# Softmax pieces of the first attention spread differently over sixteen heads, in a fused two-layer block

## The chip, the cores and the metric

One Trainium2 chip, one of its cores. The metric is the device time of the whole kernel in microseconds (us): the median of several executions. The engines of the core run side by side: TensorE (PE) with its weight load (PEld), VectorE (DVE), ScalarE (ACT), GpSimd (POOL) and SyncE (SP), which only issues DMAs here.

## The reference

Four stages follow one another on x of 8 x 256 tokens with 256 numbers each: a cross attention, a mixture of 64 experts, a second cross attention and a mixture of 8 experts. Each adds its gated result to x. The change lies in the first attention only:

```python
x = x + jnp.tanh(g_xattn[0]) * _L0_xattn_ref(_layernorm(x, axis=-1), ctx_1024, ...)
# in _L0_xattn_ref: 16 heads, D = 128, 64 keys for each of the 8 sequences
q = (hidden_states @ Wq).reshape(B, Sq, H, D)
k = (encoder_hidden_states @ Wk).reshape(B, Skv, H, D)
v = (encoder_hidden_states @ Wv).reshape(B, Skv, H, D)
q = rmsnorm(q, gq)
k = rmsnorm(k, gk)
scores = jnp.einsum('bqhd,bkhd->bhqk', q, k) * scale
attn = jax.nn.softmax(scores, axis=-1)
out = jnp.einsum('bhqk,bkhd->bqhd', attn, v)
return out.reshape(B, Sq, H * D) @ Wo
```

## The kernel before

The 2048 tokens are 16 tiles of 128; four tiles (512 tokens, two sequences) are a group, and there are four groups. `step(i)` works on group i of the first attention, i = 0 to 3. It is written once for each engine, and the engines meet at semaphores. In step i, PE, DVE, ACT and POOL make the queries and scores of group i, head by head, and between the heads the softmax, transposes and output of group i - 1. So step 0 has no softmax in it, steps 1, 2 and 3 have, and the softmax of group 3 comes after step 3 in a loop of its own, which the change leaves alone.

A head h of the loop, engine by engine, each in the order of its own program:

- PE: the q product of head h (six matmuls of 512 columns, line 1742) into one of two banks, which is free when DVE has copied head h - 2. Then, in heads that the table `turns` names, eight transposes of a tile's softmax (`transpose_attn`, line 1690), and in heads that `outs` names the output product of a tile (`output`, line 1697). Then the scores of head h - 2 (line 1727) and its row of the sum of squares (line 1718), for which POOL must have split the squares.
- DVE: the copy of the head's queries out of the bank (`qT`, line 725), then the pieces that the table `pieces` names for this head. Head 12 also has `row_stats` of the next group, head 15 `row_roots` (not in step 3).
- ACT: two squares of `qT` (lines 1372 and 1376), behind the copy; then, by its tables, `attn_out` (line 1326: two banks of transposes to `attnT`) and `exponential` (line 1322); in odd heads from 3 on it takes scores out (line 1364).
- POOL: `q2_lo`, the difference of the two squares, one subtraction a head (line 486).

The pieces of a tile j on DVE, for its 128 x 1024 scores (16 heads of 64 keys): `by_norm` (line 659: times the inverse norm), `maximum` (664), `shift` (668: less the maximum), then ACT's exponential, `sums` (673 and 675: sum and reciprocal), `divide` (682: writes `prob`, which is one buffer, so that divide j waits for the transposes of tile j - 1), and `out` (645: adds the output product to x). After the divide come PE's transposes, ACT's `attn_out` and PE's output product, and then `out`. The output product uses one bank, so output j waits for out j - 1.

The order is written out by hand in the three tables; each engine does its work in just that order, and what stands behind a waiting instruction waits too. After the sixteen heads, PE makes the last output, the keys of the next group, and its values, which ACT evacuates (lines 1315 to 1317); then the tokens of the next group are transposed, and the next step begins.

Of the kernel before, what the change touches and what calls it, by code (L numbers as in the profile page):

```python
# [101 lines left out]
def flamingo(nc, a, out, stages=4):  # L102
    with ExitStack() as ctx:
# [454 lines left out]
        def _(dve):  # L558
# [148 lines left out]
            def step(i, first_, last):  # L707
                qr.at(Q_PREP, Q_STEP, i)
                ch.at(PREP_CHAIN + STEP_CHAIN * i - (0 if first_ else SOFT_CHAIN))
                by_norm, maximum, shift, sums, divide = softmax_pieces(i - 1, (i + 1) % 2)  # L710
                t0 = T_PREP + T_STEP * i - T_HEADS + (0 if last else 2)

                def out(j):
                    residual(i - 1, j, one_bank=True)


                pieces = {0: (by_norm, 0, maximum, 0), 1: (shift, 0, by_norm, 1), 2: (maximum, 1, shift, 1),
                          3: (sums, 0), 4: (divide, 0), 5: (sums, 1), 6: (divide, 1, by_norm, 2),
                          7: (maximum, 2, shift, 2, out, 0), 8: (by_norm, 3, maximum, 3), 9: (sums, 2),
                          10: (divide, 2, out, 1), 11: (shift, 3), 13: (sums, 3), 14: (divide, 3, out, 2)}  # L720
                if not first_:

                    dve.wait_ge(s_ring.free, S_PREP + S_STEP * (i - 1) + 8)
                for h in range(H0):
                    dve.tensor_copy(qT[:, h % 3, :], qr.read(dve)[:]).then_inc(q_ring.free, 1)  # L725
                    if not first_:
                        run = pieces.get(h, ())
                        for piece, j in zip(run[0::2], run[1::2]):
                            if piece is divide:
                                divide(j, t0 + 2 * j if j else None)  # L730
                            else:
                                piece(j)
                    if h == 12 and not last:
                        row_stats(i + 1)
                    if h == 15 and not last:
                        row_roots(EPS0)
                dve.wait_ge(q_norm, 2 * i + 1)
                dve.tensor_copy(n_rows[:], n_bank[0:H0, :]).then_inc(n_copied, 1)
                if not last:
                    keys_in()  # L740
                if not first_:
                    out(3)
                dve.wait_ge(q_norm, 2 * i + 2)
                ch.add(dve.tensor_scalar(qvar[:], n_bank[:, 0:G * H0], 1.0 / D0, EPS0, ALU.mult, ALU.add))
                if not last:

                    row_apply(i + 1)
                    key_norm(1)
                    split_tokens(i + 1)
                ch.wait()  # L750
                inverse_root(rq[:], qvar[:], G * H0)
                assert first_ or last or ch.k == STEP_CHAIN, (ch.k, STEP_CHAIN)
# [535 lines left out]
        def _(act):  # L1288
# [66 lines left out]
            def step(i, first_, last):  # L1355
                qr.at(Q_PREP, Q_STEP, i)
                sr.at(S_PREP, S_STEP, i)
                tr.at(T_PREP - (0 if first_ else T_HEADS), T_STEP, i)
                if not last:
                    context_in((i + 1) % 2)  # L1360

                def scores_out(pair):
                    b = sr.read(act)
                    act.activation(raw[:, i % 2, :, 2 * pair * SKV:2 * (pair + 1) * SKV],
                                   b[:].rearrange("p (j n) -> p j n", j=G), ACT.Copy).then_inc(s_ring.free, 1)


                exps, outs = {2: 0, 3: 1, 8: 2, 12: 3}, {5: 0, 8: 1, 12: 2, 15: 3}
                for h in range(H0):
                    qr.skip(1)  # L1370
                    qr.evacuated(act)
                    act.activation(q2_hi[:, h % 3, :], qT[:, h % 3, :], ACT.Square)  # L1372

                    if not (first_ and h < 2):
                        act.wait_ge(q2_split, H0 * i + h - 1)
                    act.activation(q2[h % 2], qT[:, h % 3, :], ACT.Square).then_inc(q2_ready, 1)  # L1376
                    if not first_ and h in outs:
                        attn_out(outs[h])
                    if not first_ and h in exps:
                        exponential(i - 1, exps[h], (i + 1) % 2)  # L1380
                    if h >= 3 and h % 2:
                        scores_out((h - 3) // 2)
                scores_out(H0 // 2 - 1)
                values_in()
                if not last:
                    tokens_in()
                    keys_in()
# [235 lines left out]
        def _(pe):  # L1623
# [77 lines left out]
            def step(i, first_, last):  # L1701
                qr.at(Q_PREP, Q_STEP, i)
                sr.at(S_PREP, S_STEP, i)
                tr.at(T_PREP - (0 if first_ else T_HEADS), T_STEP, i)
                if not last:
                    context_in(i + 1)
                pe.wait_ge(xnT_ready, i + 1)
                s_bank = [None]

                def scores(h, done):  # L1710
                    qr.evacuated(pe, done - h)
                    pe.wait_ge(q2_split, H0 * i + h + 1)
                    place = [(h ^ 1) if j >= 2 else h for j in range(G)]
                    for half in range(2):
                        at, row = slice(half * 2 * P, (half + 1) * 2 * P), place[2 * half]

                        for n, v in enumerate((q2_hi, q2_lo)):
                            mm = pe.matmul(n_bank[0:H0, at], band_r[:, H0 - 1 - row:2 * H0 - 1 - row],  # L1718
                                           v[:, h % 3, at], start=(h == half == n == 0),
                                           stop=(h == H0 - 1 and half == n == 1))  # L1720
                    if h == H0 - 1:
                        mm.then_inc(q_norm, 1)
                    if h % 2 == 0:
                        s_bank[0] = sr.fill(pe)
                    for j in range(G):
                        at = (2 * j + place[j] % 2) * SKV
                        mm = pe.matmul(s_bank[0][:, at:at + SKV], qT[:, h % 3, j * P:(j + 1) * P],  # L1727
                                       kT[:, h, (j // 2) * SKV:(j // 2 + 1) * SKV], start=True, stop=True)
                    if h % 2:
                        mm.then_inc(s_ring.full, 1)  # L1730


                turns, outs = {5: 0, 8: 1, 12: 2, 15: 3}, {6: 0, 9: 1, 13: 2}
                for h in range(H0):
                    b = qr.fill(pe)
                    if first_ and h % 4 == 0:
                        pe.wait_ge(wq_split, h // 4 + 1)

                    terms = [(w, v, c) for c in range(C) for w, v in (
                        (wq_hi, xnT_top), (wq_hi, xnT_rest), (wq_lo, xnT_top))]  # L1740
                    for n, (w, v, c) in enumerate(terms):
                        mm = pe.matmul(b[:], w[:, c, h * D0:(h + 1) * D0], v[:, c, :],  # L1742
                                       start=(n == 0), stop=(n == len(terms) - 1))
                    mm.then_inc(q_ring.full, 1)
                    if not first_ and h in turns:
                        transpose_attn(i - 1, turns[h])
                    if not first_ and h in outs:
                        output(i - 1, outs[h])
                    if h >= 2:
                        scores(h - 2, h + 1)  # L1750
                scores(H0 - 2, H0)
                scores(H0 - 1, H0)
                if not first_:
                    output(i - 1, G - 1)
                if not last:
                    keys()
                pe.wait_ge(n_copied, i + 1)
                pe.sem_inc(pe_wait_done, 1)
                for j in range(G):
                    mm = pe.transpose(n_bank[:, j * H0:(j + 1) * H0], n_rows[:, j * P:(j + 1) * P],  # L1760
                                      ident[0:H0, 0:H0])
                mm.then_inc(q_norm, 1)
                values(i % 2)
                if not last:
                    transpose_xn(i + 1)
                    transpose_keys(i + 1)
# [371 lines left out]
```

## Time and profile before

| | |
|---|---|
| time, median of 3 runs | 1227.14 us (1225.15 to 1227.94) |
| the profiled execution | 1225.4 us, span 1223.6 us |
| PE busy | 951.2 us, 78% of the span |
| DVE busy | 727.4 us, 59% |
| ACT busy | 433.1 us, 35% |
| POOL busy | 279.2 us, 23% |
| heads of step 1, 2, 3 | about 100.5 to 162, 187 to 249, 273 to 335 us |

Times are counted from the start of the span. Matmuls overlap, so one instruction's duration is longer than the distance to the next one's start; distances are what an engine needs for a stretch. An idle time in brackets is that of the engine just before the instruction, with what released it. PEclk is the clock granted to TensorE, 1.00 being the full 2.4 GHz.

### The profile page before, as it was taken

The numbers are of one execution on the slowest core, as the hardware profiler recorded it, in microseconds if no ns is written. First come the engines' busy times: TensorE is split into PE (matmuls) and PEld (weight loads), VectorE is DVE, ScalarE is ACT, GpSimd is POOL, SyncE is SP. The second block draws the span as 40 slices with busy tenths as digits, with TensorE's granted clock in tenths as the row PEclk, the third lists the DMA queues.
The fourth block names the chain that finished last, engine by engine and source line by source line (L and its number), as shares of the span: only waits on it lengthen the run. The fifth ranks groups of instructions, "written<-read, shape, count | busy, mean of one in ns | idle before, by whom it ended". The sixth has DMA issues, their size and how long they took to land.

```text
span 1223.6 us, 16469 instructions
## 1 busy us (share of the span) xinstructions
PE 951.2 (78%) x5499; PEld 791.0 (65%) x5499; DVE 727.4 (59%) x1697; ACT 433.1 (35%) x811; POOL 279.2 (23%) x225
## 2 busy tenths in 40 slices
PE   5998989989977530566776756777868999999998
PEld 3876867867856320455665633443547989999898
DVE  7267567668378889322222367988986545444343
ACT  4556454455463320111111103445364233332322
POOL 0423303304200000378888730001100000000000
PEclk8999998999989765687878867888869999999899
DMA  8004000000000114388878656000000000000000
GB/s 291 4 1 148 2 1 1 1 1 1 1 0 1 44 58 106 75 185 166 179 172 183 128 130 216 1 3 1 1 1 1 1 6 13 2 17 0 18 1 18
DMA packets 58945, 66.48 MB, mean 54 GB/s; under 512 B 5069, under 2 KB 55687, under 8 KB 58119
## 3 DMA queue, kind: packets, MB, share of 16 engines
q1 hardware_dynamic: 45236, 46.45, 12.1%
q0 software_dynamic: 12288, 18.88, 8.8%
q8 instruction: 36, 0.59, 0.2%
q10 hardware_dynamic: 1363, 0.37, 0.1%
q14 instruction: 22, 0.18, 0.0%
HBM read 48.13 MB, written 17.56 MB: 54 GB/s over the span
## 4 chain that ended last, share of the span: by engine, by line
PE 46%; DVE 20%; issue 14%; POOL 7%; ACT 6%; DMA 5%; ACTq 0%; DVEq 0%; PEldq 0%; POOLq 0%; PEld 0%; SPq 0%
PE bank L2044 12%; PE bank L2070 7%; DMA acc<-y,dst_now 4%; PE bank L1742 4%; PE bank L1697 4%; POOL acc L507 3%; PE bank L1727 3%; POOL xg L497 2%; PE bank L2055 2%; PE bank L1931 2%; POOL q_lo L486 2%; DVE cand L922 2%; DVE keyT L925 2%; PE bank L1718 2%; DVE small L1067 1%
## 5 line engine op out<-in xcount | busy, mean ns | idle before, releaser
L2044 PE MATMUL bank<-gu_hi,xnT_split 128*128 128x352 f32 x640 | 164.0, 330 | 4.9 <-DVE soft L1238 3.7
L486 POOL TENSOR_TENSOR q_lo<-soft,q_hi 128x512 fp32r<-128x512 f32 x64 | 93.2, 1456 | 237.1 <-ACT soft L1376 237.0
L2044 PEld LDWEIGHTS bank<-gu_hi,xnT_split 128*128 128x128 f32 x640 | 114.6, 192 | 5.6 <-DVE soft L1238 4.0
L507 POOL DMA_INDIRECT acc<-y,dst_now x64 | 102.5, 1602 | 27.8 <-issue 20.4
L2044 PE MATMUL bank<-gu_lo,xnT_split 128*128 128x352 f32 x320 | 104.5, 327 | 0.0
L1238 DVE SCALAR_TENSOR_TENSOR soft<-sg,combine_w,bank 128x176 f32<-128x176 f32 x160 | 56.5, 395 | 70.0 <-PE bank L2044 64.5
L725 DVE COPY qT<-bank 128x512 f32<-128x512 f32 x64 | 44.2, 691 | 88.5 <-PE bank L1742 87.4
L497 POOL DMA_INDIRECT xg<-table,src_now x64 | 63.9, 999 | 127.8 <-DVE src_now L955 108.6
L975 DVE TENSOR_SCALAR y<-bank,xg 128x256 f32<-128x256 f32 x64 | 28.0, 480 | 105.0 <-PE bank L1859 105.0
L1586 ACT ACTIVATE sg<-bank 128x352 f32<-128x352 f32 x80 | 37.0, 464 | 127.3 <-PE bank L2044 123.3
L1846 PEld LDWEIGHTS bank<-xgT,w_gu 128*88 128x88 f32 x512 | 75.9, 194 | 7.4 <-issue 5.3
L1846 PE MATMUL bank<-xgT,w_gu 128*88 128x128 f32 x512 | 77.8, 317 | 0.7 <-issue 0.7
L1832 PE MATMUL bank<-ident,xg 128*128 128x128 f32 x128 | 24.9, 327 | 65.8 <-DMA xg<-table,src_now 65.8
L1434 ACT ACTIVATE xgT<-bank 128x512 f32<-128x512 f32 x32 | 19.1, 597 | 152.2 <-PE bank L1832 152.2
L1372 ACT ACTIVATE q_hi<-qT 128x512 fp32r<-128x512 f32 x64 | 40.4, 631 | 92.1 <-DVE qT L725 91.9
L2070 PE MATMUL bank<-dn_hi,actT_hi 128*128 128x256 f32 x224 | 66.8, 298 | 0.0
L2070 PE MATMUL bank<-dn_hi,actT_lo 128*128 128x256 f32 x224 | 65.9, 294 | 0.0
L2070 PE MATMUL bank<-dn_lo,actT_hi 128*128 128x256 f32 x224 | 65.5, 293 | 0.0
L1697 PE MATMUL bank<-vw,attnT 128*128 128x256 f32 x256 | 60.3, 390 | 5.6 <-ACT attnT L1326 3.5
L1727 PE MATMUL bank<-kT,qT 128*128 128x64 f32 x512 | 64.0, 268 | 0.0
L1727 PEld LDWEIGHTS bank<-kT,qT 128*128 128x128 f32 x512 | 62.5, 191 | 1.4
L1832 PEld LDWEIGHTS bank<-ident,xg 128*128 128x128 f32 x128 | 16.8, 164 | 70.6 <-DMA xg<-table,src_now 56.7
(273 smaller groups left out, 2233.8 us busy)
## 6 DMA issues: line engine op xcount, KB each, us to landing
w_gu<-in_L_ffn_w_gu SPq DMA_DIRECT2D x32, 352.0 KB
w_dn<-in_L_ffn_w_down SPq DMA_DIRECT2D x32, 176.0 KB
acc<-zeros SPq DMA_DIRECT2D x2, 2176.0 KB, 11.9
acc_rows<-acc SPq DMA_DIRECT2D x8, 512.0 KB, 5.0
gu<-in_L_gu SPq DMA_DIRECT2D x1, 3520.0 KB, 13.5
table<-xw SPq DMA_DIRECT2D x4, 640.0 KB
wo<-in_L_xattn_Wo SPq DMA_DIRECT2D x2, 1024.0 KB, 15.1
wq<-in_L_xattn_Wq SPq DMA_DIRECT2D x1, 2048.0 KB, 17.4
```

The lines of the kernel that those rows point to most:

```text
L486: pool.tensor_tensor(q2_lo[:, h % 3, :], q2[h % 2], q2_hi[:, h % 3, :], ALU.subtract).then_inc(q2_split, 1)
L497: pool.indirect_dma_start(xg[:, q, e, :], None, table, bass.IndirectOffsetOnAxis(ap=src_now[:, q, e:e + 1], axis=0)).then_inc(xg_loaded[q] ...
L507: pool.indirect_dma_start(acc[e], bass.IndirectOffsetOnAxis(ap=dst_now[:, q, e:e + 1], axis=0), y[:, q, e, :], None, compute_op=ALU.add).t ...
L725: dve.tensor_copy(qT[:, h % 3, :], qr.read(dve)[:]).then_inc(q_ring.free, 1)
L1238: ins = dve.scalar_tensor_tensor(out=act_v[:, j % 2, at:at + F1], in0=sg[:, (j + p) % 2, e * F1:(e + 1) * F1], scalar=combine_w[:, j, 2 * ...
L1697: mm = pe.matmul(o_banks[0][:, 0:DIM], attnT[:, j % 2, p, :], vw[:, j // 2, p, :], start=(p == 0), stop=(p == 7))
L1727: mm = pe.matmul(s_bank[0][:, at:at + SKV], qT[:, h % 3, j * P:(j + 1) * P], kT[:, h, (j // 2) * SKV:(j // 2 + 1) * SKV], start=True, stop ...
L1742: mm = pe.matmul(b[:], w[:, c, h * D0:(h + 1) * D0], v[:, c, :], start=(n == 0), stop=(n == len(terms) - 1))
L1832: mm = pe.transpose(b[:, at:at + P], xg[:, q, e, c * P:(c + 1) * P], ident[:])
L1846: mm = pe.matmul(b[0:I0, e * P:(e + 1) * P], w_gu[:, q, e, c, o:o + I0], xgT[:, q % 2, e, c, :], start=(c == 0), stop=(c == C - 1))
L2044: mm = pe.matmul(b[:, 0:2 * F1], v[:, c, j * P:(j + 1) * P], w[:, c, p, o, :], start=(n == 0), stop=(n == len(terms) - 1))
L2070: mm = pe.matmul(o_banks[j % 2][:, 0:DIM], v[0:n, f, :], w[0:n, f, :], start=(f == 0 and k == 0), stop=(f == FC - 1 and k == 2))
```

## The change

Three tables are rewritten. On DVE no head from 0 to 15 is without a piece any more, and norm and maximum of tiles 1, 2 and 3 come later in part. Transposes and output product of tiles 1 and 2 come a head later: transposes 1 in head 9 in place of 8 and 2 in head 13 in place of 12, outputs 1 and 2 in heads 10 and 14 in place of 9 and 13. ACT's `attn_out` moves with the transposes, and exponentials 1 and 2 go from heads 3 and 8 to 5 and 9. The work itself is the same, instruction for instruction.

```diff
@@ DVE
-                pieces = {0: (by_norm, 0, maximum, 0), 1: (shift, 0, by_norm, 1), 2: (maximum, 1, shift, 1),
-                          3: (sums, 0), 4: (divide, 0), 5: (sums, 1), 6: (divide, 1, by_norm, 2),
-                          7: (maximum, 2, shift, 2, out, 0), 8: (by_norm, 3, maximum, 3), 9: (sums, 2),
-                          10: (divide, 2, out, 1), 11: (shift, 3), 13: (sums, 3), 14: (divide, 3, out, 2)}
+                pieces = {0: (by_norm, 0), 1: (maximum, 0, shift, 0), 2: (by_norm, 1), 3: (maximum, 1, sums, 0),
+                          4: (shift, 1, divide, 0), 5: (by_norm, 2), 6: (maximum, 2), 7: (sums, 1, out, 0),
+                          8: (divide, 1, shift, 2), 9: (by_norm, 3), 10: (maximum, 3), 11: (sums, 2, shift, 3),
+                          12: (divide, 2, out, 1), 13: (sums, 3), 14: (divide, 3), 15: (out, 2)}
@@ ACT
-                exps, outs = {2: 0, 3: 1, 8: 2, 12: 3}, {5: 0, 8: 1, 12: 2, 15: 3}
+                exps, outs = {2: 0, 5: 1, 9: 2, 12: 3}, {5: 0, 9: 1, 13: 2, 15: 3}
@@ PE
-                turns, outs = {5: 0, 8: 1, 12: 2, 15: 3}, {6: 0, 9: 1, 13: 2}
+                turns, outs = {5: 0, 9: 1, 13: 2, 15: 3}, {6: 0, 10: 1, 14: 2}
```

## Rows read from the trace of the kernel before

**Rows 1.** Windows, step 1's heads: us, busy time (instructions) of each engine, PEclk, DMA.
```profile
100.50:162.00 61.50, 59.21 (x371) 50.34 (x372) 42.16 (x66) 30.23 (x55) 24.20 (x16) 1.00 0.23 75
```

**Rows 2.** Waits of PE, one answer each for steps 1, 2, 3: total, times, longest.
```profile
PE bank L1718 <- POOL q_lo L486: 2.2, 3, 1.2
...
PE bank L1718 <- POOL q_lo L486: 1.5, 2, 1.2
...
PE bank L1718 <- POOL q_lo L486: 2.1, 3, 1.2
```

**Rows 3.** Timeline of DVE in step 1, heads 2 to 5: start, duration, operation.
```profile
110.50 1.23 DVE L668 TENSOR_TENSOR raw<-raw,small 128x1024 f32 x1
111.64 0.68 DVE L725 COPY qT<-bank 128x512 f32<-128x512 f32 x1
112.25 1.21 DVE L673 TENSOR_REDUCE small<-raw 128x16 f32 x1
...
113.86 0.69 DVE L725 COPY qT<-bank 128x512 f32<-128x512 f32 x1
114.47 1.48 DVE L682 TENSOR_TENSOR soft<-raw,small 128x1024 f32<-128x1024 f32 x1
```

**Rows 4.** Timeline of POOL in step 1, the subtractions of heads 2 and 3.
```profile
110.61 2.27 POOL L486 TENSOR_TENSOR q_lo<-soft,q_hi 128x512 fp32r<-128x512 f32 x1 [0.95 <-ACT soft L1376]
113.59 1.28 POOL L486 TENSOR_TENSOR q_lo<-soft,q_hi 128x512 fp32r<-128x512 f32 x1 [0.72 <-ACT soft L1376]
```

**Rows 5.** Timeline of PE in step 1: scores 0; in head 5, product's end, transposes 0.
```profile
105.66 0.28 PE L1718 MATMUL bank<-q_hi,band_r 128*16 128x256 f32 x1 [0.63 <-POOL q_lo L486]
...
115.52 0.39 PE L1742 MATMUL bank<-xnT_top,wq_lo 128*128 128x512 f32 x1
116.01 1.09 PE L1690 MATMUL bank<-ident,soft 128*128 128x128 f32 x8
```

**Rows 6.** Timeline of PE: starts of heads 9 to 14 and transposes 2 (head 12).
```profile
130.77 0.48 PE L1742 MATMUL bank<-xnT_top,wq_hi 128*128 128x512 f32 x1
...
137.19 0.48 PE L1742 MATMUL bank<-xnT_top,wq_hi 128*128 128x512 f32 x1
...
139.94 0.48 PE L1742 MATMUL bank<-xnT_top,wq_hi 128*128 128x512 f32 x1
...
142.67 0.48 PE L1742 MATMUL bank<-xnT_top,wq_hi 128*128 128x512 f32 x1
...
144.14 1.03 PE L1690 MATMUL bank<-ident,soft 128*128 128x128 f32 x8
...
146.30 0.48 PE L1742 MATMUL bank<-xnT_top,wq_hi 128*128 128x512 f32 x1
...
152.51 0.48 PE L1742 MATMUL bank<-xnT_top,wq_hi 128*128 128x512 f32 x1
```

**Rows 7.** Timeline of DVE in step 1: out 1, copies 11 and 12, row statistics.
```profile
140.59 0.48 DVE L645 SCALAR_TENSOR_TENSOR x<-bank,gates,x 128x256 f32 x1
141.60 0.69 DVE L725 COPY qT<-bank 128x512 f32<-128x512 f32 x1 [0.53 <-PE bank L1742]
...
144.34 0.69 DVE L725 COPY qT<-bank 128x512 f32<-128x512 f32 x1 [0.92 <-PE bank L1742]
144.95 1.40 DVE L595 BATCH_NORM_STATS2 stats<-x 128x6 f32 x4
146.49 0.38 DVE L599 BATCH_NORM_AGGREGATE mv<-stats 128x2 f32<-128x6 f32 x4
```

**Rows 8.** Timeline of ACT in step 1, head 12: first square, evacuation of transposes 2.
```profile
145.06 0.63 ACT L1372 ACTIVATE q_hi<-qT 128x512 fp32r<-128x512 f32 x1 [1.10 <-DVE qT L725]
...
146.12 1.07 ACT L1326 ACTIVATE attnT<-bank 128x512 f32<-128x512 f32 x2
```

**Rows 9.** Timeline of PE at the start of step 2, first q product.
```profile
187.72 0.63 PE L1742 MATMUL bank<-xnT_top,wq_lo 128*128 128x512 f32 x1
```

**Rows 10.** Timeline of DVE after the heads of step 1: first copy of keys.
```profile
166.17 0.69 DVE L622 COPY soft<-bank 128x512 f32<-128x512 f32 x1 [4.40 <-PE bank L1633]
```

## Prediction, written before the changed kernel was timed

> **What bounds the kernel now.** I read the windows of the first attention, then TensorE's (PE's) waits there, then the timelines of VectorE (DVE), GpSimd (POOL), ScalarE (ACT) and PE over one step. The change touches only the sixteen-head loops of steps 1, 2 and 3 (step 0 has no softmax behind it). In such a loop PE is busy 59.2 of 61.5 us [rows 1], so it has little slack: a microsecond of PE idle time removed or added in it is one of the whole. PE names one releaser there: the scores of heads 0, 1 and 2 wait for POOL's subtraction q2_lo, for 2.2, 1.5 and 2.1 us in steps 1, 2 and 3 [rows 2]. POOL waits for ACT's two squares and those for DVE's copy qT of that head, and DVE is late since two softmax pieces stand between copies in heads 0 to 2. From head 4 on PE is the bound; the vector engine then waits for it.
>
> **The spacings.** On DVE a copy costs 0.61 us to the next start, a shift (as norm and divide, 128x1024) 1.14, sums with its reciprocal 1.61 [rows 3]. POOL's subtraction starts 1.95 after its head's copy (111.64 to 113.59) and takes 1.28 [rows 3, 4]. DVE's operations on two such operands and POOL's subtraction exclude each other, both ways: shift 1 from 110.50 to 111.73 makes the subtraction issued at 110.61 last 2.27; the subtraction from 113.59 to 114.87 makes divide 0, issued at 114.47, end at 115.95, 1.08 after POOL's end, in place of its 1.22. A copy beside POOL (111.64) is not lengthened. PE's head is 2.73 us plain (139.94 to 142.67), 3.63 with the transposes of a tile, 6.21 with an output product; the q product is 1.47 of it, and from the transposes to the next head it is 2.16 [rows 6].
>
> The Trainium skill has this exclusion (SBUF — State Buffer, "Who interferes with whom"): a DVE instruction with two SBUF inputs and a GpSimd instruction that reads SBUF share a port pair, and whoever issues first keeps it. The trace agrees (2.27 in place of 1.28). Without that rule the sum below would be that of the second rival.
>
> **Part 1, heads 0 to 5: waits move, little goes.** Before and after, the same eight pieces (norm, maximum, shift of tiles 0 and 1, sums 0, divide 0) and five copies come ahead of divide 0's end; only their order differs. So the copies of heads 2, 3 and 4 come earlier (one piece less by head 2's copy), and scores 1 and 2 lose most of their waits. But PE's transposes of tile 0 still stand in head 5 and wait for divide 0. They start at 116.01, 0.06 after its end (114.47 + 1.48) and some 0.26 after PE had issued its last product [rows 3, 5]. PE gets to them about 1.6 us sooner (the 2.2 of [rows 2] less the 0.63 of head 0's scores, which hang on copy 0 alone and stay [rows 5]) and waits there for that long. What remains of the gain is that divide 0 is now issued right after shift 1, ahead of POOL's subtraction, and isn't held by it: 1.48 becomes 1.22. I take 0.3 in step 1, 0.4 in step 3. In step 2 the first two products run at a low clock (0.63 us an instruction [rows 9] in place of 0.39 [rows 5]), so that copy 1 itself, now after one piece only, waits some 0.3 for PE: 0 there. ACT's exponentials have slack: exponential 1, moved from head 3 to 5, is read by sums 1 in head 7.
>
> **Part 2, heads 7 to 10.** Transposes 1 move from head 8 to 9, output 1 from 9 to 10; the work is the same. Before, the head with output 1 took 6.42 us (130.77 to 137.19) where one without a wait takes 6.21 [rows 6]: output 1 waited for ACT's evacuation of transposes 1, which stood behind the squares of head 8, and copy 8 was late behind maximum 2, shift 2 and out 0. Afterwards it stands behind copy 9, ahead of which are divide 1 and shift 2, 2.28 and a copy's 0.61 in a head of 2.73: late by 0.2 at most. Gain 0.2 a step. The moved residuals (out 0 to 2, 0.48 each [rows 7]) need output products that ended long before.
>
> **Part 3, heads 11 to 14: a new pile-up on DVE.** Before, head 11 held shift 3 alone and head 12 only the row statistics of the next group. Now head 11 has sums 2 and shift 3, and head 12 has divide 2, out 1 and the row statistics. Counted from copy 11's start (before at 141.60, which is 0.2 after PE has issued product 11: 139.94 + 1.47) [rows 6, 7]:
> - shift 3 is issued at 0.61 + 1.61 = 2.22. POOL's subtraction 11 has begun at 1.95 and ends at 3.24. Shift 3 ends 1.08 later, at 4.32. Copy 12, which PE has ready at 2.73, starts at 4.32.
> - divide 2 is issued at 4.93 and ends at 6.15. PE has issued product 13 at 2 x 2.73 - 0.2 = 5.26. Transposes 2, in head 13, start at 6.21: a new wait of 0.95.
> - out 1 at 6.06, the row statistics at 6.46. These take 2.02 (144.95 to 146.49, then 0.38 and the wait for it) [rows 7]. Copy 13 starts at 8.48; PE had its product at 5.46.
> - ACT evacuates transposes 2 behind the squares of head 13, which wait for copy 13. Before, the evacuation starts 1.78 after its head's copy (144.34 to 146.12) and takes 1.07 [rows 7, 8]: here it ends at 11.33.
> - PE: transposes 2 at 6.21, head 14 at 8.37, its product issued at 9.84. Output 2 waits for 11.38: 1.54.
> Queued behind these waits on PE are scores 11 and 12 and all that follows. Sum 2.5 us in steps 1 and 2. Step 3 has no row statistics: copy 13 starts at 6.46, the evacuation ends at 9.31, before PE comes; only the 0.95 stays.
>
> **Part 4, the end of a step.** Out 2 moves to head 15, ahead of the row roots, and puts off DVE by 0.4. DVE then idles 4.40 us for PE's key product [rows 10], which covers it; cost nothing, 0.4 a step were that cover gone. Behind the heads, PE's last output, keys, values and ACT's evacuation follow on one another, so a late head 15 passes through fully. No DMA is moved and no queue of SP touched; the load of the context waits for a transpose bank at the start of a step, long before. POOL's work is the same.
>
> **Sum.** Step 1: -0.3 - 0.2 + 2.5 = +2.0. Step 2: 0 - 0.2 + 2.5 = +2.3. Step 3: -0.4 - 0.2 + 0.95 = +0.3. Together +4.6. The profiled execution took 1225.4 us (span 1223.6), which would become 1230.0; the median of the three runs is 1.7 above it, so I state 1227.14 + 4.6 = 1231.7.
>
> **What the trace doesn't show.** The row statistics now run beside POOL's subtraction 12 (6.27 to 7.56), which they never did before. If they are held by it, copy 13 and output 2 come 1.1 later in steps 1 and 2: +2.2. If not, 0. I take 0, since the nearest row, the one-input copy at 111.64, isn't held [rows 3, 4]; below nothing it can't go, as the statistics do no less work. The Trainium skill, same section, says that a DVE instruction with at most one SBUF input doesn't contend with GpSimd, and would give 0 too.
>
> **The rivals.**
> - **Faster: the early waits really go.** Heads 1 and 2 lose their wait, 5.8 in all [rows 2] less 0.6 each in steps 1 and 3: 4.6, and output 1 gains 0.6; if nothing comes back, 1227.1 - 5.2 = 1221.9. For it: the change takes just those waits away. It decides at divide 0: its end would have to come 1.6 us sooner, and the pile of heads 11 and 12 would have to fit 5.46 us. Against it: eight pieces are eight pieces, and the pile is 8.5. Chance 0.12.
> - **No measurable change: shift 3 isn't held by POOL.** POOL is ahead by only 0.27 us. If shift 3 wins, copy 12 starts at 3.36, divide 2 ends at 5.19, before PE comes; copy 13 starts at 7.5, output 2 at 10.4 against 8.9: 1.5 in steps 1 and 2, nothing in step 3. 3.0 - 1.3 = +1.7, 1228.9. Against it: 113.59 and 114.47 show who wins when POOL is ahead. Chance 0.18.
> - **More: statistics held, or the clock.** The first gives +6.8, 1233.9. The second: PE falls to half its clock after slack stretches, as at the start of step 2 [rows 9]; ten instructions at 0.2 us more are 2.0 a time. The new waits of 0.95 and 1.5 lie close together. In two steps that is 4 more, 1235.7. Against it: the clock stood at 1.00 through step 1, with its waits of heads 0 to 2 [rows 1, 2]. Chance 0.15 for both.
> - That the change doesn't do what it says: its three tables (DVE, ACT, PE) agree with one another in order, so no.
>
> **The numbers.** My forecast gets 0.55, around 1231.7, from 1229.5 to 1233.5 alone. A measurement of this kernel can tell some 0.2% (2.5 us) from no change: the three runs lie 2.8 us apart. Clock spells that fall otherwise in later stages can take or give 2 us; so part of the forecast's weight falls below 1229.6. Slower 0.63, same 0.25, faster 0.12. The range takes in the held statistics, the clock and the unheld shift: 1225.5 to 1236.
>
> **What would show it.** The profile after: copies 2 to 4 earlier by 1.2 us and more; transposes 0 within 0.5 us of where they were, with a PE wait for divide 0 of about 1.6; shift 3 lasting over 2 us; PE waiting for divide 2 in head 13 and, in steps 1 and 2 alone, for attnT in head 14; copy 15 about 2 us later counted from copy 0 in steps 1 and 2 and about equal in step 3. I am wrong if copy 12 starts when PE has it, if ACT evacuates transposes 2 before copy 13, or if the whole shift is eaten between the steps.

## The result, and the profile after

The changed kernel takes 1239.2 us, the median of three runs (1235.5 to 1239.5): 1.0090 of the kernel before, 95% interval 1.0068 to 1.0113, so 8 to 14 us slower. A second series, with five rounds against the kernel before, gave 1.0075 (1.0055 to 1.0096), 7 to 12 us. I had forecast slower by 4.6, and a range up to 1236. The direction was right, the size less than half of the measured one.

The copies of queries (line 725) count the steps. The distance from the copy of head 0 to that of head 15, from the timelines of DVE:

| | step 1 | step 2 | step 3 | sum |
|---|---|---|---|---|
| before | 54.66 | 54.70 | 54.61 | 163.97 |
| forecast | 56.7 | 57.0 | 54.9 | 168.6 |
| after | 58.86 | 58.90 | 55.40 | 173.16 |

9.2 us of the difference is in these three loops. The profiled executions are 13.8 apart (1239.19 and 1225.4). Of the 4.6 outside the loops, 3.6 lie behind step 3, in stages whose code is the same, and the rest between and ahead of the steps. The second series fits the 9.2 of the loops alone (0.75% is 9.2 us).

Waits of PE in the heads of step 1, after: total us, times, longest. They answer to [rows 2].

```profile
PE bank L1690 <- DVE soft L682: 2.8, 2, 2.1
PE bank L1697 <- ACT attnT L1326: 1.4, 1, 1.4
PE bank L1718 <- POOL q_lo L486: 0.6, 1, 0.6
```

The waits for POOL that the kernel before had are gone but for that of head 0. In their place PE waits twice for a divide and once for ACT's evacuation. Where transposes 0 stand, the timeline of PE after, head 5 of step 1; it answers to [rows 5]:

```profile
114.11 0.39 PE L1742 MATMUL bank<-xnT_top,wq_lo 128*128 128x512 f32 x1
116.63 1.97 PE L1690 MATMUL bank<-ident,soft 128*128 128x128 f32 x8 [2.13 <-DVE soft L682]
118.25 0.56 PE L1718 MATMUL bank<-q_hi,band_r 128*16 128x256 f32 x1
118.61 0.42 PE L1718 MATMUL bank<-q_lo,band_r 128*16 128x256 f32 x1
...
119.25 1.33 PE L1727 MATMUL bank<-kT,qT 128*128 128x64 f32 x8
120.38 0.48 PE L1742 MATMUL bank<-xnT_top,wq_hi 128*128 128x512 f32 x1
```

After 2.13 us of idle time the eight transposes take 1.97 us, where [rows 5] had 1.09, and a matmul of 256 columns 0.42 where [rows 5] had 0.28. PE is at its lower level, 1.2 GHz: from 117.2 to 119.2 the granted clock is 0.50. The windows around that stretch show it in the last column but two: busy times (instructions), then PEclk, DMA share, GB/s. First before, then after, both 112 to 122 us:

```profile
112.00:122.00 10.00, 9.58 (x59) 7.89 (x58) 7.98 (x11) 7.38 (x13) 4.89 (x5) 1.00 0.36 120
```

```profile
112.00:122.00 10.00, 7.87 (x43) 6.74 (x42) 6.64 (x7) 5.10 (x9) 4.78 (x3) 0.83 0.39 129
```

What made divide 0 late, in the timeline of POOL after, subtractions of heads 1 and 2, and of DVE after; they answer to [rows 3, 4]:

```profile
106.44 2.28 POOL L486 TENSOR_TENSOR q_lo<-soft,q_hi 128x512 fp32r<-128x512 f32 x1 [0.68 <-ACT soft L1376]
109.43 1.52 POOL L486 TENSOR_TENSOR q_lo<-soft,q_hi 128x512 fp32r<-128x512 f32 x1 [0.71 <-ACT soft L1376]
```

```profile
106.34 1.22 DVE L668 TENSOR_TENSOR raw<-raw,small 128x1024 f32 x1
107.48 0.68 DVE L725 COPY qT<-bank 128x512 f32<-128x512 f32 x1
108.08 1.72 DVE L659 TENSOR_TENSOR raw<-raw,rq 128x1024 f32 x1
...
110.53 1.21 DVE L664 TENSOR_REDUCE small<-raw 128x16 f32 x1
111.99 1.22 DVE L673 TENSOR_REDUCE small<-raw 128x16 f32 x1 [0.25 <-DVE small L664]
...
115.36 1.22 DVE L682 TENSOR_TENSOR soft<-raw,small 128x1024 f32<-128x1024 f32 x1
```

Shift 0 (106.34) is issued ahead of POOL's subtraction 1 (106.44) and holds it, to 108.72. The subtraction, so pushed back, then holds norm 1, issued at 108.08, which takes 1.72 in place of 1.22. The hold is passed on.

The pile-up of heads 11 to 13, timeline of DVE after; it answers to [rows 7]:

```profile
143.54 0.69 DVE L725 COPY qT<-bank 128x512 f32<-128x512 f32 x1 [4.37 <-PE bank L1742]
144.15 1.21 DVE L673 TENSOR_REDUCE small<-raw 128x16 f32 x1
145.40 0.25 DVE L675 RECIPROCAL small<-small 128x16 f32<-128x16 f32 x1
145.68 2.18 DVE L668 TENSOR_TENSOR raw<-raw,small 128x1024 f32 x1
147.79 0.68 DVE L725 COPY qT<-bank 128x512 f32<-128x512 f32 x1
148.39 1.21 DVE L682 TENSOR_TENSOR soft<-raw,small 128x1024 f32<-128x1024 f32 x1
149.52 0.47 DVE L645 SCALAR_TENSOR_TENSOR x<-bank,gates,x 128x256 f32 x1
149.92 1.39 DVE L595 BATCH_NORM_STATS2 stats<-x 128x6 f32 x4
...
151.96 0.69 DVE L725 COPY qT<-bank 128x512 f32<-128x512 f32 x1
```

POOL beside it, the subtractions of heads 11 and 12:

```profile
145.50 1.29 POOL L486 TENSOR_TENSOR q_lo<-soft,q_hi 128x512 fp32r<-128x512 f32 x1 [4.93 <-ACT soft L1376]
149.73 1.29 POOL L486 TENSOR_TENSOR q_lo<-soft,q_hi 128x512 fp32r<-128x512 f32 x1 [2.94 <-ACT soft L1376]
```

POOL is ahead of shift 3 by 0.18, and shift 3 takes 2.18 us; copy 12 comes 4.25 after copy 11 and copy 13 at 8.42 (forecast 4.32 and 8.48). Ahead of copy 11 DVE had idled 4.37. What PE and ACT make of it, PE first, heads 13 and 14, then ACT; it answers to [rows 6, 8]:

```profile
149.66 1.09 PE L1690 MATMUL bank<-ident,soft 128*128 128x128 f32 x8 [0.67 <-DVE soft L682]
...
154.86 3.72 PE L1697 MATMUL bank<-vw,attnT 128*128 128x256 f32 x16 [1.36 <-ACT attnT L1326]
```

```profile
152.68 0.63 ACT L1372 ACTIVATE q_hi<-qT 128x512 fp32r<-128x512 f32 x1 [2.08 <-DVE qT L725]
...
153.74 1.06 ACT L1326 ACTIVATE attnT<-bank 128x512 f32<-128x512 f32 x2
```

The evacuation follows copy 13 by 1.78, as forecast. The bracket is shorter than the wait by issue times (my 0.95 and 1.54), since it begins at the end of the last matmul, not at the end of its issue. By starts of heads, 11 to 15 took 15.32 before (139.94 to 155.26) and 17.82 after (141.88 to 159.70): +2.50.

### The profile page after: what moved, and what is told of

The parts are those of the page before. It is cut to its first block, busy times and chain, and to the rows that moved or that the text cites. A ratio compares the mean times of both kernels' runs of the same rounds, so it can differ in the third digit from the quotient of the medians.

```text
span 1237.4 us, 16472 instructions
## 1 busy us (share of the span) xinstructions
PE 959.3 (78%) x5499; PEld 799.3 (65%) x5499; DVE 732.8 (59%) x1697; ACT 432.6 (35%) x811; POOL 278.3 (22%) x225
## 3 DMA queue, kind: packets, MB, share of 16 engines
q1 hardware_dynamic: 45236, 46.45, 12.1%
## 4 chain that ended last, share of the span: by engine, by line
PE 46%; DVE 20%; issue 14%; ACT 6%; POOL 6%; DMA 6%; DVEq 0%; ACTq 0%; PEldq 0%; POOLq 0%; PEld 0%; SPq 0%
PE bank L2044 12%; PE bank L2070 7%; DMA acc<-y,dst_now 5%; PE bank L1697 4%; PE bank L1742 3%; PE bank L1931 3%; POOL acc L507 2%; PE bank L1727 2%; POOL xg L497 2%; PE bank L2055 2%; POOL q_lo L486 2%; DVE cand L922 2%; DVE keyT L925 2%; PE bank L1718 1%; DVE small L1067 1%
## 5 line engine op out<-in xcount | busy, mean ns | idle before, releaser
L645 DVE SCALAR_TENSOR_TENSOR x<-bank,gates,x 128x256 f32<-128x256 f32 (+1 forms) x48 | 23.0, 482 | 67.2 <-PE bank L2070 53.0
```

## The experiments

Each is the changed kernel with nothing but the edit shown. Times are against the kernel before, run on the same chip in the same series; the loops' sum is copy 0 to copy 15 over steps 1 to 3, less 163.97. One execution of each kernel was profiled, and the steps are from it. Ratios are converted at 1227.5 us:

| kernel | ratio (95%) | in us | steps 1, 2, 3 | loops' sum |
|---|---|---|---|---|
| again_after | 1.0075 (1.0055 to 1.0096) | +9.2 | 58.89, 58.92, 55.40 | +9.2 |
| early_only | 1.0022 (1.0009 to 1.0035) | +2.7 | 56.64, 56.66, 54.79 | +4.1 |
| late_only | 1.0031 (1.0015 to 1.0047) | +3.8 | 56.91, 56.94, 55.19 | +5.1 |
| filled_wait | 1.0048 (1.0029 to 1.0067) | +5.9 | 57.29, 57.30, 55.44 | +6.1 |
| shift3_first | 1.0062 (1.0045 to 1.0079) | +7.6 | 58.04, 57.90, 54.45 | +6.4 |
| stats_h10 | 1.0040 (1.0025 to 1.0054) | +4.9 | 57.24, 57.24, 56.95 | +7.5 |
| turn0_h6 | 1.0022 (1.0007 to 1.0037) | +2.7 | 56.33, 56.29, 54.45 | +3.1 |
| both_mended | 0.9977 (0.9964 to 0.9990) | -2.8 | 53.80, 53.77, 53.52 | -2.9 |
| head5_empty | 0.9939 (0.9923 to 0.9954) | -7.5 | 52.84, 52.82, 52.58 | -5.7 |

**Once more.** 

> The changed kernel once more, as the yardstick of this series. From copy 0 to copy 15 the three steps took 58.86, 58.90 and 55.40 us in its first trace, against 54.66, 54.70 and 54.61 before: 9.2 us of the 12.1 by which the medians differ. If all the rest is a consequence of the change, this run shows +12 again (about 1239). If the rest (3 us) is the luck of clock spells and DMA in later stages, it shows +9 to +12 and the later stages of this trace differ from those of the first.

The loops repeat to 0.03 us. The medians now differ by 8.6 us, where the first series had 12.1, and the ratio equals what the loops add. So the 9.2 belong to the change; the further 3 to 5 of the first series and its trace weren't seen again in that size. Most of it lies behind step 3: the first trace spent 897.4 us there (340.0 to 1237.4), this one 894.2, the kernel before 893.8.

**The early part alone.**

```diff
-  4: (shift, 1, divide, 0), 5: (by_norm, 2), 6: (maximum, 2), ...         # pieces
+  4: (shift, 1, divide, 0), 5: (sums, 1), 6: (divide, 1, by_norm, 2), ... # from 5 on as before
-  exps, outs = {2: 0, 5: 1, 9: 2, 12: 3}, {5: 0, 9: 1, 13: 2, 15: 3}
+  exps, outs = {2: 0, 4: 1, 8: 2, 12: 3}, {5: 0, 8: 1, 12: 2, 15: 3}
-  turns, outs = {5: 0, 9: 1, 13: 2, 15: 3}, {6: 0, 10: 1, 14: 2}
+  turns, outs = {5: 0, 8: 1, 12: 2, 15: 3}, {6: 0, 9: 1, 13: 2}
```

> Only heads 0 to 4 are as in the change (with exponential 1 in head 4); from head 5 on everything is as before. Theory A (the wait of transposes 0 for divide 0 grew to 2.1 us, and behind it PE runs at half clock for some 3.4 us): copy 0 to copy 15 gets 1.9 longer in steps 1 and 2 (0.4 for divide 0, 1.5 for the clock) and 0.3 in step 3, +4.1 in all, about +0.3%. Theory B (the clock falls there for another reason, or the pile-up of heads 11 and 12 feeds it): 0.4 longer a step, +1 in all, not to be told from no change. Theory C (the purpose of the change, early waits really go): shorter by 1 or more a step.

It came out at +1.98, +1.96 and +0.18, theory A to a tenth. The windows of 112 to 122 us show the fallen clock with nothing of the late part in the kernel, and PE's wait the same 2.1:

```profile
112.00:122.00 10.00, 7.87 (x44) 6.67 (x43) 6.98 (x9) 5.84 (x11) 4.68 (x3) 0.83 0.48 158
```

```profile
PE bank L1687 <- DVE soft L682: 2.1, 1, 2.1
```

**The late part alone.**

```diff
-  pieces = {0: (by_norm, 0), 1: (maximum, 0, shift, 0), 2: (by_norm, 1), 3: (maximum, 1, sums, 0), 4: (shift, 1, divide, 0), ...
+  pieces = {0: (by_norm, 0, maximum, 0), 1: (shift, 0, by_norm, 1), 2: (maximum, 1, shift, 1), 3: (sums, 0), 4: (divide, 0), ...
-  exps = {2: 0, 5: 1, 9: 2, 12: 3}
+  exps = {2: 0, 3: 1, 9: 2, 12: 3}
```

> Heads 0 to 4 as before, heads 5 to 15 as in the change. Theory A: the pile-up of sums 2, shift 3, divide 2, out 1 and the row statistics costs PE the waits in heads 13 and 14, some 2.3 us from copy 0 to copy 15 in steps 1 and 2 and 0.5 in step 3, +5.1 in all, about +0.4%; PEclk stays 1.00 in step 1. Theory B (the clock belongs to the late part): +8 or more, with PEclk under 1.00 in step 1.

+2.25, +2.24, +0.58, and PEclk 1.00 in step 1. Early and late sum to 9.2, just what both cost together: two causes that don't touch each other. Theory B of either run is out.

**The clock by itself.**

```diff
-            def transpose_attn(i, j):
+            def transpose_attn(i, j, filler=0):
+                b0 = tr.fill(pe)
+                for _ in range(filler):
+                    pe.matmul(b0[:], wq_hi[:, 0, 0:P], xnT_top[:, 0, :], start=True, stop=True)
                 pe.wait_ge(attn_ready, G * i + j + 1)
-                    b = tr.fill(pe)
+                    b = tr.fill(pe) if g else b0
-                        transpose_attn(i - 1, turns[h])
+                        transpose_attn(i - 1, turns[h], 8 if turns[h] == 0 else 0)
```

> The changed kernel, with eight more matmuls of 512 columns (1.9 us) ahead of PE's wait for divide 0 in head 5; they write to the bank that the transposes overwrite, so nothing computed changes. PE does more work here, and no wait is shortened. Theory A (the slack of 2.1 us lets the clock fall): the clock stays up, copy 5 to copy 6 takes 4.0 us in place of 5.6 in steps 1 and 2, and the kernel gets 3 us faster than the changed one, about 1236. Theory B (the clock falls whatever PE does there): no gain, or a loss of up to 1.9 a step.

The timeline of PE of this kernel, step 1:

```profile
114.85 1.99 PE L1684 MATMUL bank<-xnT_top,wq_hi 128*128 128x512 f32 x8
117.14 1.09 PE L1690 MATMUL bank<-ident,soft 128*128 128x128 f32 x8 [0.30 <-DVE soft L682]
```

The transposes start no earlier against copy 0 (14.11 us behind it in both), but take 1.09 again. Copy 5 to copy 6 is 4.02, 4.03 and 4.09, where the changed kernel had 5.57, 5.64 and 4.10. More work on PE made steps 1 and 2 1.6 us shorter each; step 3, where the clock had not fallen, stayed. So what the low clock costs there is 1.6 a step, and it comes of PE standing idle. The measured ratio fell by 0.27 points, 3.3 us.

**The hold on shift 3.**

```diff
-  11: (sums, 2, shift, 3)
+  11: (shift, 3, sums, 2)
```

> The changed kernel with shift 3 ahead of sums 2 in head 11; the sum of work is the same. If POOL's hold on shift 3 (2.18 us in place of 1.22) is what makes copy 12 and divide 2 late, copy 11 to copy 12 takes 3.4 in place of 4.25, PE's wait for divide 2 in head 13 goes (0.7), and the wait for attnT in head 14 stays near 1.4 to 1.5 as copy 13 is still held back by the row statistics: copy 11 to copy 15 is 16.8 in steps 1 and 2 (17.8 in the changed kernel) and 15.3 in step 3 (16.2). If only the amount of work in heads 11 and 12 counts, all three stay as they are.

The timeline of DVE, head 11, of this kernel:

```profile
143.85 0.69 DVE L722 COPY qT<-bank 128x512 f32<-128x512 f32 x1 [4.37 <-PE bank L1739]
144.46 1.22 DVE L668 TENSOR_TENSOR raw<-raw,small 128x1024 f32 x1
...
147.22 0.69 DVE L722 COPY qT<-bank 128x512 f32<-128x512 f32 x1
```

Shift 3 takes 1.22, copy 12 follows after 3.37, and PE has no second wait for a divide. Copy 11 to 15 is 16.95, 16.94 and 15.22 (17.84, 17.83 and 16.19 in the changed kernel). The same pieces in the other order are worth 0.9 a step. The time alone (1.0062) would not show it beside 1.0075.

**The row statistics.**

```diff
-                    if h == 12 and not last:
+                    if h == 10 and not last:
                         row_stats(i + 1)
```

> The changed kernel with the row statistics of the next group in head 10 in place of head 12. If the wait for attnT comes of the copy of head 13 standing behind the statistics, it goes: copy 11 to copy 15 is 16.2 in all three steps (17.8, 17.8 and 16.2 in the changed kernel), 3 us less in all. The rival, that ACT is late for a reason of its own (exponential 3 ahead of it), leaves 17.8.

Copy 11 to 15 became 16.18 and 16.17 in steps 1 and 2, and stayed at 16.17 in step 3: the wait for attnT was the statistics' alone. But copy 5 to copy 6 of step 3, which the edit can't touch, took 5.68 in place of 4.10. The windows, here and in the changed kernel, at the wait of transposes 0 in step 3 (1.9 us long in both):

```profile
288.00:298.00 10.00, 8.12 (x45) 6.92 (x44) 6.71 (x8) 5.32 (x10) 4.90 (x3) 0.83 0.00 0
```

```profile
294.00:304.00 10.00, 8.11 (x51) 6.95 (x50) 8.14 (x9) 5.83 (x11) 4.72 (x3) 1.00 0.01 2
```

So a wait of the same length lets the clock fall in one kernel and not in the other. In the five kernels with this wait (changed, again_after, early_only, shift3_first, stats_h10) it fell behind 11 of 15: behind all ten of steps 1 and 2 (2.12 to 2.14 us), and behind one of the five of step 3 (1.87 to 1.90).

A second wait says that length alone doesn't decide. Between the steps PE waits for ACT's `xnT`, 2.64 to 2.65 us in every kernel. First the kernel before, between steps 1 and 2, and then shift3_first at the same place:

```profile
182.68 1.09 PE L1641 MATMUL bank<-ident,soft 128*128 128x128 f32 x8 [2.65 <-ACT xnT L1333]
184.00:190.00 6.00, 5.46 (x18) 4.05 (x19) 2.58 (x12) 2.58 (x7) 0.00 (x0) 0.55 0.00 0
```

```profile
186.56 1.09 PE L1638 MATMUL bank<-ident,soft 128*128 128x128 f32 x8 [2.65 <-ACT xnT L1330]
188.00:194.00 6.00, 5.52 (x27) 4.24 (x28) 4.26 (x13) 3.52 (x8) 0.26 (x1) 1.00 0.00 0
```

The clock fell in the first and stood in the second (and in stats_h10). From copy 15 of step 1 to copy 0 of step 2 these two spent 32.74 and 30.98 us in the same code. So falls of the clock also make up to 2 us of difference between kernels outside the loops.

**Transposes 0 a head later.**

```diff
-  7: (sums, 1, out, 0), 8: (divide, 1, shift, 2), ...
+  7: (sums, 1), 8: (divide, 1, shift, 2, out, 0), ...
-  attn_out = {5: 0, 9: 1, 13: 2, 15: 3}         # ACT's outs
+  attn_out = {6: 0, 9: 1, 13: 2, 15: 3}
-  turns, outs = {5: 0, 9: 1, 13: 2, 15: 3}, {6: 0, 10: 1, 14: 2}
+  turns, outs = {6: 0, 9: 1, 13: 2, 15: 3}, {7: 0, 10: 1, 14: 2}
```

> The changed kernel with transposes 0 a head later (6), output 0 in head 7 and out 0 in head 8. Divide 0 ends before PE comes, so the wait of 2.1 us goes and with it the fall of the clock: copy 0 to copy 15 takes 55.2 in steps 1 and 2 (58.9 in the changed kernel) and 53.5 in step 3 (55.4), 9 us less in all, about 1228. If the clock falls in that stretch without the wait too, 56.7 in steps 1 and 2.

Half a miss: 56.33, 56.29 and 54.45. The clock stayed up and the 2.1 went, but a new wait came for output 0:

```profile
PE bank L1694 <- ACT attnT L1323: 1.0, 1, 1.0
```

**Both causes mended**: turn0_h6, with `10: (maximum, 3, shift, 3), 11: (sums, 2)` and the row statistics in head 10.

> Transposes 0 in head 6 as in the run before it, and in addition shift 3 and the row statistics in head 10, where DVE idled 4.4 us behind maximum 3. If the two causes are the whole of the loss, no wait but that of head 0's scores (0.6) is left: copy 0 to copy 15 takes 52.7 in all three steps, 2.0 less than before the change in each, 6 us less in all, about -0.5% against the kernel before. If something else takes the place of the removed waits, 54 to 55 and no gain over the kernel before.

53.80, 53.77, 53.52: 0.8 to 1.1 above what I expected, by that same wait (1.0 us in steps 1 and 2, 0.7 in step 3), and no other is left but that for head 0's scores. It is faster than the kernel before, 0.9977 (0.9964 to 0.9990). Why output 0 waits, in its timelines, DVE and then ACT:

```profile
117.19 1.71 DVE L659 TENSOR_TENSOR raw<-raw,rq 128x1024 f32 x1
119.02 0.69 DVE L722 COPY qT<-bank 128x512 f32<-128x512 f32 x1
```

```profile
119.78 0.62 ACT L1369 ACTIVATE q_hi<-qT 128x512 fp32r<-128x512 f32 x1
120.30 0.62 ACT L1373 ACTIVATE soft<-qT 128x512 f32<-128x512 f32 x1
120.83 1.07 ACT L1323 ACTIVATE attnT<-bank 128x512 f32<-128x512 f32 x2
```

Norm 2 in head 5 is held by POOL, copy 6 is late, and ACT's evacuation stands behind the squares that wait for it.

**Head 5 left empty.**

```diff
-  5: (by_norm, 2), 6: (maximum, 2), 7: (sums, 1), ...
+  6: (by_norm, 2), 7: (sums, 1, maximum, 2), ...
-  exps = {2: 0, 5: 1, 9: 2, 12: 3}
+  exps = {2: 0, 6: 1, 9: 2, 12: 3}
```

> The run with both causes mended kept a wait of 1.0 us of output 0 for attnT: norm 2 in head 5, held by POOL (1.71 us), put off copy 6, ACT's squares and the evacuation behind them. Here head 5 has no piece; norm 2 is in head 6, maximum 2 in head 7, exponential 1 in head 6. If that chain is the cause, the wait goes and copy 0 to copy 15 takes 52.8 us in all three steps (53.8, 53.8, 53.5 in the run before it; 54.7 before the change): about 5.5 us less in all than before the change, -0.4 to -0.5%. If ACT is late for the evacuation by its own work, 53.8 stays.

52.84, 52.82 and 52.58, as expected, at 1219.9 us (1217.9 to 1220.8): 0.9939 of the kernel before (0.9923 to 0.9954), 7 us faster. All waits of PE in step 1 between 100 and 162 us:

```profile
PE bank L1715 <- POOL q_lo L486: 0.6, 1, 0.6
PE bank L1626 <- ACT kT L1304: 0.5, 2, 0.3
```

It uses the changed kernel's order of heads 0 to 4. With that order the waits of heads 1 and 2 are gone and nothing has come in their place; what it needed was that the next in line, transposes 0, move along with it.

## Why the prediction was wrong in size

- **What bounds the kernel** was read rightly: PE's idle time in the loops is the time. In all kernels of the table but one the loops' sum lies inside the measured interval. The exception is stats_h10 (7.5 in its trace, 3.1 to 6.6 measured). Its trace has a third fall of the clock, worth 1.6, that its other executions need not have had; they were not profiled, so this stays open.
- **Part 1 failed, in two terms.** First, "divide 0 ... isn't held by it: 1.48 becomes 1.22" was right as to divide 0, yet norm 1 and sums 0 were then late: the subtraction of head 1, pushed back by shift 0, reached into norm 1 (+0.5), and maximum 1 to sums 0 took 1.46 (+0.2). Transposes 0 started 0.4 later against copy 0 (13.74 to 14.11), where I had them 0.3 earlier: +0.7 in step 1. This term is read from the timelines; no run takes the passed-on hold away by itself. It shows in a sign that I had named, too: copies 2 and 3 came 1.4 and 2.0 earlier against copy 0, but copy 4 only 0.5, where I had written 1.2 and more. Second, and larger, I priced the wait "of about 1.6" as idle time alone. It was 2.1 (PE came 1.66 sooner, as forecast, and the transposes 0.4 later), and behind it the clock fell: from the start of transposes 0 to that of head 6 it took 3.75 in place of 2.21, +1.5 in each of steps 1 and 2.
- **The rival of the clock** had the right price (2.0 a time forecast, 1.5 measured) and was put at the wrong wait: I looked at heads 13 and 14, whose waits of 0.7 and 1.4 let nothing fall in any of the kernels that had them in the profiled steps, and not at head 5, where part 1 itself had created the longest wait of the loop. It also stood at 0.15, shared. My reason against it, that the clock stood through the waits of heads 0 to 2, compared 1.2 us with 1.6; no wait as long stood in the old loop to vouch for it. Outside the loop the trace before did have a warning: the low clock of [rows 9] stands behind the wait of 2.65 us for `xnT` shown above.
- **Part 2 was right:** heads 6 to 11 took 0.22 less (21.72 to 21.50), forecast 0.2.
- **Part 3 was right:** 2.50 measured in step 1 and 2.5 forecast, 0.87 and 0.95 in step 3, with each link: shift 3 held, divide 2 late, the statistics ahead of copy 13, ACT behind it. shift3_first and stats_h10 took single links away and found their prices, 0.9 and 1.65.
- **Part 4 was right in kind.** The loops' loss passes through fully. From copy 15 to the next copy 0 the changed kernel took a further 0.3 and 0.5 us, not forecast. Over the profiled kernels the distance between steps 1 and 2 runs from 30.98 to 33.03 with the granted clock (1.00 to 0.90), and that between steps 2 and 3 from 30.78 to 31.46, so these two can't be put down to the change.
- **The unseen cost**, row statistics beside POOL: 1.39 after, 1.40 before. Nothing, as taken.
- **The rival of an unheld shift 3** needed shift 3 to overtake POOL, whose lead I had put at 0.27. The lead was 0.18, and it was enough: shift 3 took 2.18. The faster rival had the effect right and the place wrong: the early waits did go, and head5_empty shows that they can stay away, with transposes 0 in head 6.

In numbers, the loops' 9.2 against the forecast 4.6, by early_only, late_only and filled_wait: the clock 3.2, forecast 0; the rest of part 1 +0.9, the later start of transposes 0 in the three steps, forecast -0.7; parts 2 and 3 together +5.1, forecast +5.3. What the first series had beyond 9.2 stays open. It lay mostly in later stages and was not there in the second.

## What to carry to other kernels

When waits are removed ahead of a join, find what the join waits for: here transposes 0 waited for the eighth piece, and another order of the eight changes only which of them are held, so the transposes have to move. Price a concentrated wait twice, once as idle time and once for what PE's clock does behind it; if the trace shows no wait as long in that loop at full clock, the second price belongs in the sum. And follow a hold between two engines for more than one hop, as the operation pushed back holds the next one.

## What the runs showed of the hardware

The wait of 1.9 to 2.1 us between stretches of dense matmuls was followed by a fall of the granted clock in 11 of 15 cases; waits of 1.2 to 1.4 us in the same loops by none of the profiled ones. With eight dummy matmuls in the wait (three cases) or the wait gone (turn0_h6, both_mended, head5_empty) there was none at this place. At the wait of 2.65 us between steps 1 and 2 the clock fell in nine of the eleven profiled kernels, at the one between steps 0 and 1 in none.

The Trainium skill (TensorE: Matmul & The Clock Gate, section "Why this matters for your kernels") advises against idle gaps of PE between bursts of matmuls that are longer than any of these. Here shorter ones were enough, and not always, and the measurement decides.

DVE's operations on two SBUF operands and POOL's subtraction held each other in whichever order they were issued (POOL 2.28 for 1.28 behind shift 0, DVE 1.72 for 1.22 behind POOL), while the row statistics, with one operand, ran beside POOL's subtraction of 149.73 at their old 1.39.
